# Multiplying layers 2 and 3 of the first chunk as plain fp32 in a compressed interaction network

## What is computed

```python
for (W, b), split in zip(conv_params, split_flags):        # W1, W2, W3; True, True, False
    h = x.shape[1]
    z = jnp.einsum('bhd,bmd->bhmd', x, x0).reshape(B, h * x0.shape[1], D)
    xk = jax.nn.relu(jnp.einsum('oc,bcd->bod', W, z) + b[None, :, None])
    if split:
        half = xk.shape[1] // 2
        x, xk = (xk[:, :half], xk[:, half:])
    results.append(xk)
pooled = jnp.sum(jnp.concatenate(results, axis=1), axis=2)
return pooled @ Wo.T + bo
```

## The kernel before

| q | layer, chunk | step |
|---|---|---|
| 0 | layer 1, chunk 0 | 0 |
| 1 to 4 | layer 2, chunk 0 | 1 |
| 5 | layer 1, chunk 1 | 1 |
| 6 to 9 | layer 3, chunk 0 | 2 |
| 10 | layer 1, chunk 2 | 2 |
| 11 to 14 | layer 2, chunk 1 | 2 |
| 15, 16 ... | layer 1 of chunk 3, then layer 2 of chunk 2 | 3 |

## Time and profile before

### The profile page before, as it was taken

How to read it: one execution, slowest core, us unless ns; L and a number is a source line. 1 busy time by engine, 2 the same in 40 slices (tenths; PEclk the granted TensorE clock), 3 DMA queues, 4 the chain that set the end, 5 groups by cost and what they waited for, 6 DMA issues and landing times.

```text
span 465.0 us, 6018 instructions
## 1 busy us (share of the span) xinstructions
PE 454.0 (98%) x1620; PEld 304.6 (66%) x1620; DVE 420.6 (90%) x486; ACT 318.7 (69%) x398; POOL 413.5 (89%) x152
## 2 busy tenths in 40 slices
PE   8998699999999999999999999999999999999997
PEld 3355366766767676776767677776767767677774
DVE  0495888999999999999999999999999999999997
ACT  2584766867768586876858687676868768677661
POOL 0458597999989899898999989898999999899995
PEclk9999999999999999999999999999999999999999
DMA  8899987998977949596894959689595953822100
GB/s 203 226 231 222 216 180 165 213 233 178 219 158 170 234 102 226 120 227 140 178 228 107 230 114 224 137 188 218 122 233 106 228 125 86 186 45 47 28 17 1
DMA packets 22784, 75.66 MB, mean 163 GB/s; under 512 B 5843, under 2 KB 5843, under 8 KB 18548
## 3 DMA queue, kind: packets, MB, share of 16 engines
q1 hardware_dynamic: 22772, 75.52, 74.3%
HBM read 59.51 MB, written 0.00 MB: 128 GB/s over the span
## 4 chain that ended last, share of the span: by engine, by line
PE 81%; POOL 7%; DMA 4%; DVE 3%; ACT 3%; SPq 1%; issue 1%; DVEq 0%; POOLq 0%
PE y_ps L826 25%; PE y_ps L832 15%; PE y_ps L814 14%; PE y_ps L816 14%; PE y_ps L822 7%; POOL zl L589 7%; PE y_ps L838 3%; DMA a_rep<-x_sb 2%; DVE z L632 2%; DMA shifted<-xt_dram 1%; PE y_ps L791 1%; ACT zh L493 1%; PE y_ps L818 1%; PE y_ps L834 1%; PE zx_ps L758 0%
## 5 line engine op out<-in xcount | busy, mean ns | idle before, releaser
L589 POOL TENSOR_TENSOR zl<-z,zh 128x1024 fp32r<-128x1024 f32 (+1 forms) x141 | 403.9, 2899 | 33.2 <-ACT zh L493 33.0
L632 DVE TENSOR_TENSOR z<-a_ps,b_fac 128x512 f32<-128x512 f32 (+2 forms) x256 | 271.9, 1085 | 27.0 <-PE y_ps L838 12.3
L493 ACT ACTIVATE zh<-z 128x1024 fp32r<-128x1024 f32 (+1 forms) x141 | 176.2, 1251 | 115.3 <-DVE z L632 115.0
L832 PE MATMUL y_ps<-zl,w_high 128*128 128x512 f32 x330 | 152.5, 555 | 3.2 <-POOL zl L589 3.2
L814 PE MATMUL y_ps<-zh,w_high 128*128 128x512 f32 x330 | 130.5, 396 | 3.9 <-ACT zh L493 3.9
L816 PE MATMUL y_ps<-zh,w_low 128*128 128x512 f32 x330 | 129.1, 391 | 0.0
L826 PE MATMUL y_ps<-z,w_raw 128*128 128x512 f32 x252 | 128.4, 591 | 0.0
L832 PEld LDWEIGHTS y_ps<-zl,w_high 128*128 128x128 f32 x330 | 61.6, 188 | 72.1 <-issue 59.4
L814 PEld LDWEIGHTS y_ps<-zh,w_high 128*128 128x128 f32 x330 | 61.9, 188 | 19.1 <-issue 3.1
L816 PEld LDWEIGHTS y_ps<-zh,w_low 128*128 128x128 f32 x330 | 62.1, 188 | 13.9 <-issue 0.2
L826 PEld LDWEIGHTS y_ps<-z,w_raw 128*128 128x128 f32 x252 | 47.3, 188 | 10.4
(11 more groups left out here) (54 smaller groups left out, 192.3 us busy)
## 6 DMA issues: line engine op xcount, KB each, us to landing
b_fac<-xt_dram SPq DMA_DIRECT2D x52, 512.0 KB, 8.7
shifted<-xt_dram SPq DMA_DIRECT2D x64, 256.0 KB, 4.9
a_rep<-x_sb SPq DMA_DIRECT2D x91, 128.0 KB, 2.4
shifted<-xt_dram SPq DMA_DIRECT2D x64, 128.0 KB, 5.2
b_fac<-xt_dram SPq DMA_DIRECT2D x16, 256.0 KB, 10.1
a_rep<-x_sb SPq DMA_DIRECT2D x62, 64.0 KB, 2.1
w_raw<-w_dram SPq DMA_DIRECT2D x2, 640.0 KB, 5.9
w_raw<-w_dram SPq DMA_DIRECT2D x2, 384.0 KB, 6.7
```

Source lines behind the costliest of these rows:

```text
L493: nc.scalar.activation(zh[:, slot, 0:end - native, :], z[:, slot, native:end, :], ACT.Copy).then_inc(zh_ready, 1)
L589: nc.gpsimd.tensor_tensor(zl[:, slot, 0:end - native, :], z[:, slot, native:end, :], zh[:, slot, 0:end - native, :].bitcast(F32), ALU.subtract
L632: return nc.vector.tensor_tensor(dst, factor.unsqueeze(1).to_broadcast(list(dst.shape)), others, ALU.mult)
L832: mm = nc.tensor.matmul(y, wh[layer][:, w, :], zl[:, slot, t, :], start=False, stop=end_here)
```

## The change

Six more groups are native: the second half of layer 2 of chunk 0 (q 3 and 4) and layer 3 of chunk 0 (q 6 to 9). q 0, 1 and 2 were native already; layer 1 of chunk 1 (q 5) stays split. The counts of the split semaphores are taken over (`splits_before`), PE waits for the second part of the raw weights in the groups that read it, and its waits for the low weight parts move to the first split groups. ScalarE, which has no zh of these groups any more, gets two waits: for `b0_made` before `x_to_psum(1)`, and for `z_ready` of q 7 before `a_to_psum(2, 0, 1)`. GpSimd makes both parts of layer 3's low weights ahead of its first subtraction, where they stood between its subtractions.

```diff
-NATIVE_GROUPS = 3
+NATIVE = (0, 1, 2, 3, 4, 6, 7, 8, 9)
...
 def is_native(q):
-    return isinstance(q, int) and q < NATIVE_GROUPS
+    return isinstance(q, int) and q in NATIVE
...
+def splits_before(q):
+    return q - natives_before(q)
+
+def natives_before(q):
+    return sum(n < q for n in NATIVE) if isinstance(q, int) else len(NATIVE)
...
                         if pos == 4:
+                            act.wait_ge(b0_made, 2 * GT)
                             x_to_psum(1)
                             round_w(3, 1)
...
                         if pos == 7:
+                            act.wait_ge(z_ready, groups_before(2) + 2)
                             a_to_psum(2, 0, 1)
                             x_to_psum(2)
...
                 for k, (pos, layer, g, q, e) in enumerate(steps(i)):
+                    if i_is(i, 1) and pos == 4:
+                        split_w(3, 0)
+                        split_w(3, 1)
                     if is_native(q):
                         continue
-                    if i_is(i, 1) and pos == 4:
-                        split_w(3, 0)
-                    if i_is(i, 2) and pos == 5:
-                        split_w(3, 1)
...
-                    pool.wait_ge(zh_ready, q - NATIVE_GROUPS + 1)
+                    pool.wait_ge(zh_ready, splits_before(q) + 1)
...
-                            pe.wait_ge(w_loaded[layer][0], 16)
+                            pe.wait_ge(w_loaded[layer][g // 2], 16)
...
-                    if layer == 2 and i_is(i, 1) and g == 2:
+                    if layer == 2 and i_is(i, 2) and g == 0:
                         pe.wait_ge(w_split[2], 2)
-                    if layer == 3 and i_is(i, 2) and g in (0, 2):
-                        pe.wait_ge(w_split[3], g // 2 + 1)
+                    if layer == 3 and i_is(i, 3) and g == 0:
+                        pe.wait_ge(w_split[3], 2)
```

More of the change, by code:

```diff
@@ L126, in dve_tiles_before @@
 def dve_tiles_before(i):
-    if isinstance(i, int) and (i < 2 or i > NCHUNK):
+    if isinstance(i, int) and (i < 3 or i > NCHUNK):
         return sum(by_dve for k in range(i) for *_, by_dve in dve_tiles(k))
-    return i * DVE_PER_ITER + (sum(by_dve for k in range(2) for *_, by_dve in dve_tiles(k)) - 2 * DVE_PER_ITER)
+    return i * DVE_PER_ITER + (sum(by_dve for k in range(3) for *_, by_dve in dve_tiles(k)) - 3 * DVE_PER_ITER)
 def dve_tiles(i):
@@ L790, in body @@
                             weights = w_raw[layer][:, (natives + splits).index((g, t)), :]
-                            mm = nc.tensor.matmul(y, weights, z[:, slot, t, :], start=(g == 0 and t == 0), stop=False)
+                            mm = nc.tensor.matmul(y, weights, z[:, slot, t, :], start=(g == 0 and t == 0),
+                                                  stop=(layer > 1 and g == GROUPS[layer] - 1 and t == GT - 1))
                         if layer == 1:
@@ L811, in body @@
                     x_weights = splits.index((g, X_TILE[layer])) if by_dve else None
-                    pe.wait_ge(zh_ready, q - NATIVE_GROUPS + 1)
+                    pe.wait_ge(zh_ready, splits_before(q) + 1)
                     for t, w in places:
@@ L828, in body @@
                     last = g == GROUPS[layer] - 1
-                    pe.wait_ge(zl_ready, q - NATIVE_GROUPS + 1)
+                    pe.wait_ge(zl_ready, splits_before(q) + 1)
                     for t, w in places:
```

## The result

The changed kernel takes 464.49 us (median of 13 runs, 463.48 to 466.49) against 467.32 for the kernel before on the same chip; the ratio is 0.9949, 95% interval 0.9936 to 0.9962. In a second set, beside the experiments, it took 464.40 (ratio 0.9945, 0.9930 to 0.9960). By the ratios that is 2.4 to 2.6 us (2.8 and 2.2 by the medians), where the forecast's sum had 1.6.

A forecast was written before the change was run, and what follows sets the result against it. The prediction took the start-up as bound by the split groups' path to TensorE and by the loads. The profiled 466.92 less 1.6 us of lead gave 465.3, 465.5 by the median; it took 465.4, range 464.6 to 467.0.

The forecast's parts named there:

- the forecast's sum: Whole run: 466.92 less a lead of 1.6 us gives 465.3; by the median 465.5, taken as 465.4.
- What bounds: Start-up: split groups' way through DVE, ScalarE, GpSimd, PE, and loads; q 10 stays tied to the landing at 53.15.
- q 3 to q 9 on TensorE: Native groups: q 5 begins at 36.43, q 6 at 40.2, q 8 at 48.75; PE free at 55.6, then stands 1.2.
- The price of a native group: On PE, four tiles take 8 x 0.43 = 3.43 us against 2.93 split; six groups add 3.0 us.
- q 12's zl: PE waits some 1.5 us for it, done at 66.98; q 13 begins at 67.8, PE's lead shrinking to 1.7 us.
- VectorE's lead: q 14 begins on DVE at 65.32 instead of 66.91, q 15 at 69.6 instead of 71.22: 1.6 us early.
- both hold, with about a microsecond to spare: Before q 15: chunk 3's x lands at 66.3, chunk 2's a_rep by 67.7; ScalarE wants them at 68.6 and 69.1.
- Afterwards: From q 15 on: engines run 1.6 early; PE's lead falls from 1.7 to the smaller near 101.95, with about 0.34 wait.
- don't follow their issue by 0.3 us: Rival at 46.89 and 53.15: landings and q 10 move 0.3 earlier, giving 465.0, at the far end 462.4; chance 0.08.
- the lead wasn't given back near 95: Rival: ScalarE's a_rep landing at 94.92 stays, PE waits 1.8 near 101.95, time 466.9; chance 0.13.
- TensorE wasn't slower: Rival: PE's clock falls in pauses before q 8 and q 10; q 8 and q 9 take 13.7, time 469.3; chance 0.07.
- The rule that the prediction took from the Trainium skill: PE's pauses: waiting for DMAs lets the clock go back to 1.2 GHz, speaking against native groups that end early.

The follow-up runs named there:

- after_again: The changed kernel run once more with no edit, beside the experiments: 464.40 us, ratio 0.9945 to the kernel before.
- q12_too: Changed kernel with one more native group, q 12 (second of layer 2, chunk 1): 464.82 us, ratio 0.9957 to the kernel before.
- The loads experiments: Early a_rep spreads issued half a b_fac sooner: on the changed kernel 465.08 us, with chunk 3's x also earlier 465.22; on the kernel before 467.38.
- fetch_after: Changed kernel plus five one-column matmuls, result unread, in TensorE's pause at q 12: 465.45 us, ratio 0.9973 to the kernel before.
- q9_native: Against the changed kernel, only q 9 of the six new groups is native: 465.21 us, ratio 0.9955 to the kernel before.
- l2_native: Only the change's layer-2 part: q 3 and 4 native, q 6 to 9 split: 467.81 us, ratio 1.0026 to the kernel before.
- l3_native: Only the change's layer-3 part: q 6 to 9 native, q 3 and 4 split: 465.41 us, ratio 0.9972 to the kernel before.
- loads_before: Kernel before, with the two early a_rep spreads each issued half a b_fac sooner: 467.38 us, ratio 1.0016 to the kernel before.
- early_before: Kernel before, with the first half of chunk 1's b_fac issued ahead of SyncE's wait for b0_picked: 464.12 us, ratio 0.9942.

## Why the prediction was right, step by step

- **What bounds** (the loads near 53 us and the split groups ahead of q 10): right. q 10 begins on VectorE at 54.26 (forecast 54.3) and on TensorE at 56.72 (56.8); no zh or zl of q 3, 4 and 6 to 9 is waited for.
- **q 3 to q 9 on TensorE**: later than worked out in this execution, whose granted clock was 0.50 to 0.72 between 8 and 20 us. q 5 began at 37.08 (forecast 36.43) and q 6 at 41.05 (40.2); in after_again, at 1.00, they began at 36.35 and 40.33. q 8 began at 49.26 (48.75), behind a spread half that landed at 47.24 (46.89). The price of a native group held (7.06 and 7.10 us for two, where 2 x 3.43 was reckoned; 8 x 0.43 is 3.44). The delay cost nothing, as q 10 is tied to the load; ahead of q 10 TensorE waited 0.35 us, not 1.2.
- **q 12's zl**: TensorE waited 1.05 us (forecast 1.5), at 66.93, and began q 13 at 67.74 (forecast 67.8). In q12_too the pause taken away brought nothing that its profile shows.
- **VectorE's lead**: forecast 1.6 at q 14 and at q 15. At q 14 it is right (65.24 against 66.91, 1.67). At q 15 it is 1.34 (71.22 - 69.88). The step that failed in part is "both hold, with about a microsecond to spare": chunk 2's spread half landed at 68.70 and not at 67.7, ScalarE waited 0.22 us for it, and VectorE stood 1.70 instead of 1.37 us ahead of q 15. The loads experiments show that this landing is the next bound at once.
- **Afterwards**: here the sum was mis-sized. It let TensorE's lead of 1.7 us fall to VectorE's lead near 100 and stay there. TensorE's first matmuls of q 13, q 18 and q 24, before and after, show another course:

```profile
69.53 0.39 PE L814 MATMUL y_ps<-zh,w_high 128*128 128x512 f32 x1
...
84.77 0.40 PE L814 MATMUL y_ps<-zh,w_high 128*128 128x512 f32 x1
...
102.77 0.40 PE L814 MATMUL y_ps<-zh,w_high 128*128 128x512 f32 x1
```

```profile
67.74 0.39 PE L827 MATMUL y_ps<-zh,w_high 128*128 128x512 f32 x1
...
83.40 0.39 PE L827 MATMUL y_ps<-zh,w_high 128*128 128x512 f32 x1
...
100.94 0.39 PE L827 MATMUL y_ps<-zh,w_high 128*128 128x512 f32 x1
```

The lead is 1.79 at q 13 and falls to 1.37, VectorE's 1.34, at q 18 already: TensorE comes early to q 17's zl, and q 17 takes 3.30 us (80.10 to 83.40) where a group of layer 2 or 3 takes 2.92. Near 100 the lead rises again, to 1.83: there q 23 takes 3.39 us in the kernel before (99.38 to 102.77) and 2.93 in the changed one. From q 15 on VectorE to q 24 the way thus became 0.5 us shorter (31.06 for 31.55), which lies in no term of the prediction. With fewer instructions on TensorE (four matmuls for ten in a native group) an instruction fetch comes later and falls behind a load, no longer into it; fetch_after shows what that is worth.
- **What was luck.** The 1.8 us between the two profiled spans are 1.6 of VectorE's waits, less 0.3 for the landing, plus 0.5 for the fetch. The two misses nearly cancel, so that the closeness of the number is in part luck; the 1.6 itself is not.
- **The rest of the 2.4 to 2.6 us**, 0.6 to 0.8, is not seen in the profiled pair; 1.8 is 0.4%, the end of the interval (0.9962). The profiled execution of after (465.27) lies 0.8 above the median of its kernel, that of before (466.92) 0.4 below. Either the landings are on the whole earlier in the changed kernel, which one profile a kernel can't tell, since they move by half a microsecond between executions; or the fetch costs more in other executions than in the profiled ones, as the 1.1 to 1.3 us of fetch_after suggest, though q9_native, with a fetch on the load, has 0.9955. It stays open.
- **The rivals.** The landings stayed (53.15 and 53.02), so they don't follow their issue by 0.3 us; the lead wasn't given back near 95, as that wait went away; and the granted clock stayed 1.00 behind the pauses of 1.15 and 0.35 us (q 8 and 9 took 7.10 us for 16 passes, 0.44 apiece), so TensorE wasn't slower. The rule that the prediction took from the Trainium skill (TensorE: Matmul & The Clock Gate, HAM oscillation — how this bites in real kernels), that waiting for loads lets the clock fall, did not show at these pauses.

## What to carry to other kernels

When an engine is freed in a start-up, look for the next landing and ask whether it follows its issue or the bytes ahead of it: here a transfer issued 3.4 us earlier landed 1.1 us later, and only filling a hole in the stream brought it forward. Here the one split right ahead of the tied step cost about as much as all six together, so try the last group first. A pause of the bound engine is worth something only where nothing later waits for the same thing: here 1.05 us taken away brought nothing that the profile or the median shows.

## What the runs showed of the hardware

A load on which an instruction fetch falls lands later. The 16 KB on queue 8 follow the length of TensorE's program: five small matmuls more, and the fetch comes at 89.0 instead of 93.5. Where it falls into the four 512 KB pieces, they take 13.0 to 13.4 us from the first issue to the last landing (before, l2_native, l3_native, q9_native, loads_before, early_before, fetch_after), elsewhere 12.0 to 12.7 (the other seven). In one of these, q12_too, the fetch at 89.7 meets only the last piece; that one is on time, but the spread half behind it lands 2.3 us later instead of 1.0, and TensorE's 0.61 us near 100 follow. So 16 KB, which at the 215 GB/s of this stretch are under a tenth of a microsecond, made a load about 1 us late, and q 24 0.5 us. By the Trainium skill (Runtime: NRT & Kernel Launch, Instruction fetch mechanics) instructions come in blocks of 16 KiB over a DMA queue of the engine's own, at a cost that is mostly hidden; the size agrees, and for TensorE itself no wait shows, but the loads beside it pay. The packet itself takes 1.4 us (1.1% of 16 engines' 8 us in the row above), about what the load is late; that the one makes the other isn't shown.
